# Mixing and routing skewed by single sequences, and a new order of the first loads, in a two-layer transformer kernel

## What is computed

```python
A = jnp.maximum(jnp.abs(masked.sum(axis=0)), 1.0)      # summed over all sequences
O = jnp.einsum('hst,bthe->bshe', A, V).reshape(b, s, dim)
Y = (O - mu) / jnp.sqrt(var + GN_EPS) * gn_gamma + gn_beta
x = x + (jax.nn.relu(x_normed @ wg_w) * Y) @ wo_w
...
h = _layernorm(x, axis=-1)
probs = jax.nn.softmax(h @ gate_weight.T, axis=-1)
top_v, top_i = jax.lax.top_k(probs, 2)                 # weights normalised over the two
out = x + sum(weight * (silu(gate) * up) @ down)       # of the two chosen experts
```

## Time and profile before

| | us |
|---|---|
| three runs | 1836.09, 1837.38, 1838.32; median 1837.38 |
| the profiled execution: time, span | 1832.11, 1830.3 |
| busy in the span: TensorE, VectorE, ScalarE, POOL | 1352.7, 1266.0, 657.9, 224.3 |

### The profile page before, as it was taken

How to read it: one execution, slowest core, us unless ns; L and a number is a source line. 1 busy time by engine, 2 the same in 40 slices (tenths; PEclk the granted TensorE clock), 3 DMA queues, 4 the chain that set the end, 5 groups by cost and what they waited for, 6 DMA issues and landing times.

```text
span 1830.3 us, 37451 instructions
## 1 busy us (share of the span) xinstructions
PE 1352.7 (74%) x14566; PEld 1024.7 (56%) x14566; DVE 1266.0 (69%) x2529; ACT 657.9 (36%) x1533; POOL 224.3 (12%) x375
## 2 busy tenths in 40 slices
PE   1886878687768777877787778867886656639996
PEld 0664656456655655665566555745674444426664
DVE  3877687769776967796778677877877657643332
ACT  2233423532343334323423343344233422313442
POOL 1000001000100010001000000010000015623333
PEclk9896789778868886888598759875886567669998
DMA  9910000000000000000000000000000034313332
GB/s 317 333 44 1 8 14 2 1 19 3 1 1 19 3 1 1 19 3 1 1 19 3 1 1 20 2 1 1 8 1 1 1 140 165 124 56 51 61 60 41
DMA packets 51245, 70.82 MB, mean 39 GB/s; under 512 B 4912, under 2 KB 46576, under 8 KB 49520
## 3 DMA queue, kind: packets, MB, share of 16 engines
q1 hardware_dynamic: 43904, 58.83, 10.0%
q0 software_dynamic: 7152, 9.38, 3.1%
HBM read 34.52 MB, written 33.67 MB: 37 GB/s over the span
## 4 chain that ended last, share of the span: by engine, by line
issue 66%; PE 15%; DVE 8%; POOL 4%; ACT 3%; DMA 2%; POOLq 0%; SPq 0%; DVEq 0%; ACTq 0%
PE ps L900 11%; POOL rstd L1337 3%; POOL rstd L1336 1%; DMA out<-ptf 1%; PE ps L904 1%; DVE experts L675 1%; PE ps L472 1%; ACT big L1256 1%; PE ps L1002 1%; DMA ptf<-in_spread 1%; PE ps L398 1%; DVE ptf L1509 1%; ACT experts L517 0%; PE ps L445 0%; DMA kf<-in_dn 0%
## 5 line engine op out<-in xcount | busy, mean ns | idle before, releaser
L1256 ACT ACTIVATE big<-ps,st 128x128 f32<-128x128 f32 x768 | 205.6, 407 | 205.6 <-DVE st L1590 205.6
L1002 PE MATMUL ps<-ident,big 128*128 128x128 f32 x1024 | 183.7, 347 | 34.6 <-ACT big L1256 18.3
L1509 DVE TENSOR_TENSOR ptf<-ps,ptf 128x1024 f16<-128x1024 f32 x128 | 154.4, 1221 | 64.7 <-ACT ptf L1262 63.4
L1002 PEld LDWEIGHTS ps<-ident,big 128*128 128x128 f32 x1024 | 163.0, 185 | 61.4 <-ACT big L1256 31.7
L1336 POOL TENSOR_TENSOR rstd<-mv,eps 128x1 f32<-128x1 f32 x80 | 18.4, 229 | 1274.4 <-DVE mv L1400 1274.4
L1262 ACT ACTIVATE ptf<-ps 128x1024 f16<-128x1024 f32 x128 | 130.6, 1031 | 88.9 <-PE ps L1002 88.8
L1588 DVE TENSOR_REDUCE st<-ps 128x8 f32<-128x1024 f32 x96 | 117.0, 1218 | 35.5 <-PE ps L900 35.5
L900 PE MATMUL ps<-wo,qhl 128*128 128x256 f32 x512 | 119.6, 388 | 15.4 <-DVE qhl L1514 13.2
L900 PEld LDWEIGHTS ps<-wo,qhl 128*128 128x128 f32 x512 | 96.0, 192 | 32.9 <-issue 15.2
L900 PE MATMUL ps<-experts,ptf 128*128 x312 | 100.4, 383 | 0.0
L1242 ACT ACTIVATE qhl<-big 128x1024 f16<-128x1024 f32 x32 | 33.8, 1057 | 162.9 <-DVE big L1474 160.6
(11 more groups left out here) (318 smaller groups left out, 3469.5 us busy)
## 6 DMA issues: line engine op xcount, KB each, us to landing
scratch<-blank SPq DMA_DIRECT2D x10, 1950.0 KB, 18.9
big<-in_gu SPq DMA_DIRECT2D x8, 1024.0 KB, 7.5
ptf<-scratch SPq DMA_DIRECT2D x39, 130.0 KB, 2.0
kf<-in_dn SPq DMA_DIRECT2D x8, 512.0 KB, 8.2
xin<-in_x SPq DMA_DIRECT2D x16, 128.0 KB, 2.2
cin<-in_ctx SPq DMA_DIRECT2D x16, 128.0 KB, 2.6
big<-in_wq SPq DMA_DIRECT2D x2, 1024.0 KB, 6.4
wo<-in_wo SPq DMA_DIRECT2D x1, 2048.0 KB, 13.9
```

The costliest lines, as they stand in the source:

```text
L1002: m = pe.transpose(ps_f(u, j // 4, P, (j % 4) * P), big[u][:, j * P:(j + 1) * P], ident[:])
L1256: m = f(big[u][:, c], ps_all[u][:, c], ACT.Exp, scale=scale, bias=st32[u][:, 3, j:j + 1])
L1509: S(u, tt(pt_l[u][:, c], ps_all[u][:, c], pt_h[u][:, c], ALU.subtract), f"pt{n}l{h}")
```

## The change

Four things are changed.

1. The loads are issued in a new order: key and value weights, biases and spread table, four constants, both sequences' inputs, then the query weights with the rotary tables and sinks on a semaphore of their own (`wq_in`). ScalarE and VectorE split the small weights first. ScalarE rounds the query weights after the constants and ahead of its table load. VectorE takes their remainders, with the scaling of the sinks, ahead of `k0` in the start of the turns, and TensorE waits for them ahead of `a20`.
2. Mixing and routing run over 17 steps, a new sequence at each step and its later stages a step behind. In step t TensorE runs the mix of t+1, transposes t, transposes the normalised row of t-1, then the output products of t and the gate products of t-1. The choice of experts still takes four sequences together (steps 5, 9, 13 and after the last), the slots a step later.
3. The parcels have four sets of places, partly in the buffer of the last expert, so that a set is used again only two groups later; the last expert is loaded early, but rounded by ScalarE after the steps and its remainder taken by VectorE after the blocks. Sends go by sequence, one in each of steps 7 to 14, two in 15 and 16, four at the end. Experts 0 to 6 are split in single steps (`WEIGHTS_HIGH`, `WEIGHTS_LOW`).
4. The places' copies follow the choice of experts, and some semaphores are merged (`ready`, `w_high`, `b_slots`).

The core of the diff:

```diff
-            load(big[0][:], A["wq"][:, 0, :], "w_in")
-            load(big[1][:], A["wq"][:, 1, :], "w_in")
             load(kf[0][:], A["wk"], "w_in")
             load(kf[1][:], A["wv"], "w_in")
             load(ptf[0][0:64, 0:1152], A["b0"], "w_in")
             load(ptf[1][0:64, 0:1152], A["spread"], "w_in")
...
+            load(ident[:], A["ident"])
             load(xn[0][:], A["mask"])
             load(memw[:, 0:1], A["memw"].to_broadcast([P, 1]))
+            load(rows[:, BO, :], A["rows"][BO:BO + 1, :].to_broadcast([P, DM]))
+            rows_of_x(0)
+            rows_of_x(1)
+            load(big[0][:], A["wq"][:, 0, :], "wq_in")
+            load(big[1][:], A["wq"][:, 1, :], "wq_in")
+            for t, n in [(cosI, "cosI"), (sinI, "sinI"), (sinkT, "sinkT")]:
+                load(t[:], A[n], "wq_in")
...
+            act.wait_ge(sig("wq_in"), 5 * 16)
+            for n in range(2):
+                f(wq_h[:, n, :], big[n][:], ACT.Copy).then_inc(sig("w_high"), 1)
             act.preload_act_table_set("exp_and_others")
...
+            def queries_ready():
+                dve.wait_ge(sig("wq_in"), 5 * 16)
+                link(ts(sinkT[:], sinkT[:], 1.0 / SCALE0, None, ALU.mult))
+                for n in range(2):
+                    dve.wait_ge(sig("w_high"), 3 + n)
+                    last = tt(wq_l[:, n, :], big[n][:], wq_h[:, n, :], ALU.subtract)
+                last.then_inc(sig("ready"), 1)
...
+            all_turns(pe, Own(pe, "pe_own", 0), TENSOR_TURN, stages, turn, later, ("a20", queries_ready))
...
+            all_turns(dve, own, VECTOR_TURN, stages, turn, later, ("k0", queries_ready))
```

Mixing and routing on TensorE, ScalarE, VectorE, POOL and SP (in this order):

```diff
+        STEPS = NSEQ + 1
+        WEIGHTS_HIGH = {0: 0, 1: 1, 2: 2, 3: 3, 6: 4, 7: 5, 10: 6}
+        WEIGHTS_LOW = {1: 0, 2: 1, 3: 2, 4: 3, 7: 4, 8: 5, 11: 6}
+        def sends_at(t):
+            return {7: (0,), 8: (1,), 9: (2,), 10: (3,), 11: (4,), 12: (5,), 13: (6,), 14: (7,),
+                    15: (8, 9), 16: (10, 11)}.get(t, ())
...
+            mixed(0)
+            for t in range(STEPS):
+                if t + 1 < NSEQ:
+                    mixed(t + 1)
+                if t >= 6 and t % 4 == 2:
+                    ranked(t // 4 - 1)
+                if t < NSEQ:
+                    turned(t, "b_atr", "b_a", af_b[t % 4])
+                if t >= 1:
+                    turned(t - 1, "b_tr5", "b_ln5", parcel[(t - 1) // 4][0][(t - 1) % 4])
+                if t < NSEQ:
+                    projected(t)
+                if t >= 1:
+                    gated(t - 1)
...
+            for t in range(STEPS):
+                if t >= 6 and t % 4 == 2:
+                    gate_exp(t // 4 - 1)
+                if t < NSEQ:
+                    out_of_psum(t, "b_atr", "b_aT")
+                if t >= 1:
+                    out_of_psum(t - 1, "b_tr5", "b_xT5")
+                    first, second = [parcel[(t - 1) // 4][k][(t - 1) % 4][:, 0:DM] for k in range(2)]
+                    f(second, first, ACT.Copy).then_inc(sig("b_twin"), 1)
+                if t in WEIGHTS_HIGH:
+                    w_high(WEIGHTS_HIGH[t])
             gate_exp(BTURNS - 1)
+            w_high(NE - 1)
...
+            for t in range(STEPS):
+                if t < NSEQ:
+                    mixed(t)
+                if t >= 1:
+                    added(t - 1)
+                if t < NSEQ:
+                    attended(t)
+                if t >= 1:
+                    normed_rows(t - 1)
+                if t >= 5 and t % 4 == 1:
+                    routed(t // 4 - 1)
+                if t >= 6 and t % 4 == 2:
+                    slots_of(t // 4 - 1)
+                if t in WEIGHTS_LOW:
+                    w_low(WEIGHTS_LOW[t])
+                if t >= 1:
+                    logits(t - 1)
+            routed(BTURNS - 1)
             slots_of(BTURNS - 1)
...
+            cp(blocks[:], block_f[:]).then_inc(sig("b_slots"), 1)
+            w_low(NE - 1)
...
+            for t in range(STEPS):
+                if t < NSEQ:
+                    root(t, "g", 2)
+                if t >= 1:
+                    root(t - 1, "5", 0)
+                for n in sends_at(t):
+                    send(n)
+            for n in range(12, NSEQ):
+                send(n)
...
+            for t in range(STEPS):
+                if t + 4 < NSEQ:
+                    columns(t + 4)
+                if t in WEIGHTS_LOW and WEIGHTS_LOW[t] + 2 < NE:
+                    e = WEIGHTS_LOW[t]
+                    sp.wait_ge(sig(f"w{e % 2}_lo"), e // 2 + 1)
+                    load(e % 2, e + 2)
```

More of the change, by code:

```diff
@@ L120, with all_turns @@
          "a21", "a22", "a23", "a3m", "a30", "a31", "a32", "a33", "T00", "T01", "a50", "a51", "a52", "a53"}
-def all_turns(eng, own, order, stages, turn, later=None):
+def all_turns(eng, own, order, stages, turn, later=None, before=()):
     order = [(int(item[0]), item[1] == "+", item[2:]) for item in order.split()]
@@ L129, in all_turns @@
         if ahead:
+            if before and name == before[0]:
+                before[1]()
+                before = ()
             if later and name not in FIRST:
@@ L133, in all_turns @@
             stages[name](u)
+    if before:
+        before[1]()
     if later:
@@ L328, in program, with runs @@
         PER = {"act": 0, "pool": 14, "pool_b": 12, "dve": 144, "dve_b": 44, "dve_c": 26}
[L332 to L337, removed]
+        def runs(space, first, last):
+            m = last - first
+            return space[:, first * RW:last * RW].rearrange("p (u c) -> p u c", c=RW), m
+        rows_f, spare = rows[:].rearrange("p i d -> p (i d)"), experts[:, NE - 1, 0:16 * RW].bitcast(F32)
+        kf_f = kf[0][:].rearrange("p a n -> p (a n)")
+        tails = [(x[:, None, 1560:1560 + RW], 1) for x in ptf]
+        sets = [[[runs(rows_f, 0, 4)], [runs(rows_f, 4, 6)] + tails],
+                [[runs(spare, 0, 4)], [runs(spare, 4, 8)]],
+                [[runs(rows_f, 0, 4)], [runs(rows_f, 4, 6)] + tails],
+                [[runs(big[0][:], 0, 4)], [runs(big[0][:], 4, 7), runs(kf_f, 0, 1)]]]
+        parcel = [[[x[:, i, :] for x, m in part for i in range(m)] for part in group] for group in sets]
         stage_gu = [b[:] for b in big]
@@ L389, in ranked @@
                 m.then_inc(sig("b_ranks"), 1)
[L391 to L434, removed]
@@ L506, in gate_exp, with out_of_psum @@
                 gap = gate_w[:, 0, 4 * it:4 * it + 4]
-                act.wait_ge(sig("gate_gap"), it + 1)
+                act.wait_ge(sig("b_chosen"), it + 1)
                 f(gap, gap, ACT.Exp).then_inc(sig("gate_exp"), 1)
[L510 to L529, removed]
+            def out_of_psum(n, ready, done):
+                u = n % 4
+                act.wait_ge(sig(ready, u), at(ready, n // 4, u))
+                f(aT_b[u], ps_b(u, 1, DM), ACT.Copy).then_inc(sig(done, u), 1)
@@ new lines, in vector_b @@
+            for part in sets[1]:
+                for x, m in part:
+                    mark(dve.memset(x[:, :, PLACE + 1:RW], 0.0))
+            own.wait()
+            for t in range(STEPS):
[15 more added lines that the diff above has]
+                    logits(t - 1)
```

286 lines of the change are left out of this document (146 added, 140 removed).

## The result

The changed kernel took **1796.59 us** (median of 4 runs, 1792.72 to 1799.61) beside 1837.07 us for the kernel before (4 runs, 1836.09 to 1838.32): ratio 0.9778, 95% interval 0.9758 to 0.9798, 40.5 us less by the medians. The forecast was 1803.0 us in 1789 to 1817: right in direction and range, 6 us short of the gain. The profiled execution took 1792.72 us (span 1790.9), 39.4 us less than the span before.

The account below looks back on a forecast made before the run. It took mixing and routing as bound by round trips, no engine full, and the opening by load order. Gains of 14.0 and 22.2 less 1.8 us made 34.4, so 1803.0 us for the runs, range 1789 to 1817.

Parts of the forecast that it names:

- Opening: Stretch before the first product: small weights loaded and split first, first copy out of PSUM at 24.3 us; 14.0 us gained.
- Mixing and routing: First statistics of mixed rows to last logits: 115.5 us instead of 137.7; 22.2 us gained, between 16.9 and 30.9.
- The term that was mis-sized: Mixing and routing: TensorE's mean granted clock taken as the present 0.69, 0.38 of the way up, giving 115.5 us.
- The step model: Mixing and routing: a step's stages summed, 7.4 us at 1.2 GHz, 5.7 at 2.4; whole part 120.8 or 106.8 us.
- floor forecast 7.0: Mixing and routing: steps with an expert's remainders or a choice of experts cannot be under 7.0 us.
- Tail: After the last logits: the last expert's remainders hold a scatter, column copies stand ahead; 1.8 us lost, bounds 0 and 3.7.
- POOL and the queues: Mixing and routing: work moved past queues costs nothing, POOL's two roots a step (0.19 + 0.55 us each) returning in time.
- Only the opening pays: Rival, mixing and routing: single-file steps cost 8.6 us as before, only the opening less the tail gained; 1825.2 us, chance 0.07.
- the opening doesn't do what it says: Rival, opening: small weights land with the query weights or ScalarE's later wait eats the gain; 1817.0 us, chance 0.06.
- The serial chain: Rival, mixing and routing: a step's work runs one after the other, 13.2 us a step; 1898 us, chance 0.03.
- The fourth: Rival, mixing and tail: a clock that stays up and a small tail give more than the range; chance 0.03.

Follow-up runs that it names:

- opening_only: The kernel before with only the new opening (order of the loads, query weights' copies and remainders behind the small weights'): 1822.78 us, ratio 0.9922.
- after_busy: The changed kernel with unused filler products on TensorE behind each step's mix (20 or 6): 1794.84 us, ratio 0.9772.
- skew_only: The changed kernel with the opening of the kernel before: 1813.45 us, ratio 0.9866.
- the later logits: The changed kernel with VectorE's copy of the logits one step later, behind the next row's statistics: 1795.73 us, ratio 0.9789.
- before_busy: The kernel before with unused filler products on TensorE, 44 ahead of the first transpositions and 38 behind the output products: 1833.04 us, ratio 0.9975.
- tail_twice: The changed kernel with the last expert's two remainder subtractions made twice: 1797.53 us in its one run.
- before_full: The kernel before with more unused filler products on TensorE (66, 58, and 5 between transpositions): 1831.49 us, ratio 0.9974.
- early_tail: The changed kernel with ScalarE's query-weight wait and copies behind its first PSUM copies, and the last expert's wide subtraction in step 16: 1792.86 us, ratio 0.9765.

## Why the prediction was right, and where it was off

*Opening, 14.0 us forecast, 14.6 measured.* Each step held: small weights there at 9.0 us (8.3 forecast), the query weights at 18.65 (19.3), then two copies and the table load with no gap, first copy out of PSUM at 23.67 (24.3). The remainders of the queries ran from 25.54 to 30.0 us, under keys and values, as forecast, and the queries began at 33.30 us, straight behind the values. opening_only gives the gain alone, 15.5 us (10.8 to 17.8 by its interval).

*Mixing and routing, 22.2 us forecast, 26.6 measured.* **The term that was mis-sized is the clock**: "The mean clock now, 0.69, is 0.38 of the way up; with it 115.5 us." It was taken over from the old order without a reason, and the clock came out at 0.87. TensorE's pauses had changed, from 5.6 us and more ahead of a round's first transposition to 3.4 us and less; that this raised the clock is likely, not shown. The step model itself held: between its ends (120.8 us at 1.2 GHz, 106.8 at 2.4 GHz) 0.87 gives 110.4 us, measured 111.15; 0.96 gives 107.9, after_busy measured 108.13; 0.85 gives 111.0, skew_only 112.71. Single steps too: with fill-in 6.84 us (floor forecast 7.0), without at full clock 5.76 (5.7). Within a step the mean clock is too coarse: step 12 took 7.08 us at 0.76, where the model gives 6.5. What I got right was that most of the gain is cover, 23.2 of 26.6 us at like clock. What I read wrongly was the wait that the old order had: "the engine that produced a stage waits for the last of the four" is not its largest, VectorE's 18.3 us for ScalarE's copies of the experts is.

*Tail, 1.8 us lost forecast, 0.6 measured.* One scatter was held, as forecast, but for 1.90 us, not 2.41: 0.94 us over the others. The four small column copies cost nothing; they stand in VectorE's wait for ScalarE's exponential, and the first of the eight scatters even begins 0.35 us sooner after the last logits (6.23 instead of 6.58 us). The Trainium skill's page "SBUF — State Buffer", section "Who interferes with whom", has a probe in which `tensor_tensor` did not stall GpSimd's DMAs. The runs here differ: doubling these subtractions held a second scatter (2.01 us), moving the wide one away released all eight (0.96 us).

*POOL and the queues* cost nothing, as forecast: VectorE waits for no root behind a scatter, though a few scatters in the steps took 2.0 to 2.3 us. The 0.19 us of a root's first instruction holds for the one of two groups that is listed there; in the other, roots beside an expert's remainders took 1.08 and 2.15 us before. In the changed kernel none did.

*The rivals.* "Only the opening pays" and "the opening doesn't do what it says" fall by skew_only and opening_only. The reason for the first, a clock that stays at 0.50 whenever TensorE has paused, is more than the earlier trace rows show, and the changed kernel contradicts it: it pauses in every step and ran steps 2 to 4 at 1.00. The serial chain would have shown steps of 13.2 us and decides from 9.4; the longest step is 8.4 (step 1, with the first expert's fill-in behind an empty start). The fourth, a clock that stays up with a small tail, was given 0.03, and it is the one that came nearest: both happened, only not at their extremes, so the time stayed in the range. It deserved more.

*The sum.* In the profiled executions 39.4 against 34.4 us: 4.4 from the clock's term, 1.2 from the tail, 0.6 from the opening, less 1.2 us that the stretches left alone, turns and experts, were longer. That the median of the runs gained 40.5 adds 1.1 us that no term explains.

## What to carry to other kernels

When a change reorders the work of TensorE, don't carry the mean granted clock over: cost the step at both levels and keep both as bounds; which of them the new order will get could not be told here from the length of its pauses (next section). Before a part is called bound by round trips, add up by cause what its busiest engine waits for: the 18.3 us stood in one line of the waits. Ask of each wait placed in an engine's queue what stands behind it (3 us of this opening were lost to a wait that the first copy did not need). And moving a wait later helps only if what it waits for is not also late for another reason: the later logits gave 1.7 us alone, and in the last steps nothing until the clock was held.

## What the runs showed of the hardware that was not expected

Useless products can pay: with fillers the old order's part fell by 6.4 us and the new order's by 3.0. And the same pause can be followed by either level of the clock. TensorE of the changed kernel, in steps 2 and 8:

```profile
1475.79 0.44 PE L415 MATMUL ps<-ident,ptf 128*128 128x128 f32 x2 [3.06 <-DVE ptf L684]
...
1516.11 0.69 PE L415 MATMUL ps<-ident,af 128*128 128x128 f32 x2 [3.05 <-DVE af L684]
```

Pauses of 3.05 or 3.06 us lie ahead of the transpositions in each of steps 2 to 4, where the granted clock is 1.00 throughout (1472.52 to 1493.07 us); behind the pause of step 8 it is 0.50 (1516.10 to 1520.12), and the two transposing products take 0.69 instead of 0.44 us. In before_busy pauses of 0.84 and 0.93 us were followed by slow output products (3.24 and 3.29 us). What decides between the two was not found.

In all thirteen traces a scatter that begins inside a wide subtraction ends 0.83 to 0.87 us after that subtraction, however long it had left: in the changed kernel 1583.67 + 1.90 = 1585.57 us with the subtraction's end at 1584.74, and 1517.13 + 2.28 = 1519.41 us with the end at 1518.57; in tail_twice 1593.90 and 1593.07; in the kernel before 1531.01 + 2.41 = 1533.42 us with the end at 1532.58. One that begins 0.05 us ahead of it takes 0.97 us. So the forecast's 2.41 us was a matter of when the scatter begins, not a fixed price. The same section of the Trainium skill says that a VectorE instruction with two SBUF inputs and a GpSimd instruction that reads SBUF exclude each other and that the one issued first keeps the port to its end; the runs agree with that, with 0.83 to 0.87 us to finish after it. Whether the narrow subtraction (128x1024, 1.22 us) holds a scatter was not seen, since none began well inside it; it does hold a root on POOL, which in the kernel before took 1.08 instead of 0.19 us beside it (1519.84 us).

In these traces the old opening is also the less steady one: ScalarE's first copy of the weights began at 16.61 us in the kernel before, but at 18.93, 17.70 and 19.40 us in before_busy, before_full and skew_only, which load in the same order, and the first copy out of PSUM at 38.3 to 41.1 us; with the new order it began at 23.7 to 23.9 us in six traces. That fits the 15.5 us of opening_only, a little over the 14.6 of the two profiled executions; the interval of the 15.5 us is too wide to show it.

The turns between, with the same instructions in all these kernels, took from 1429.4 us (early_tail, first copy out of PSUM at 21.21 to the mix's last scaling at 1450.63) to 1436.0 us (after_busy, 23.77 to 1459.79). A few microseconds of the whole time are therefore no evidence on a part, and the verdicts above rest on the parts' own rows. What makes this spread was not tried.
